# Exponentials of half the heads straight from PSUM, with the negated row maximum as bias, in every attention tile

## The chip, the core and the metric

The kernel runs on one core of a Trainium2 chip. Five engines work side by side, each through its own queue of instructions in order: TensorE (PE in the rows; PEld is its loading of weights), VectorE (DVE), ScalarE (ACT), GpSimd (POOL) and SyncE (SP), which here issues most transfers. They wait for each other by semaphores. The metric is the device time of one execution in microseconds, taken as a median of runs.

## The reference

A recurrent attention layer (gated linear attention, in chunks) is followed by two layers of local attention, each with a feed-forward part. The change touches the softmax of the local attention alone, here cut to what matters (16 windows of 64 rows in each of 2 batches, 8 heads of 64):

```python
q = l2norm(q) * qs; k = l2norm(k) * ksc
q, k = rotary_xpos(q, k)
sim = jnp.einsum('bhwid,bhwjd->bhwij', bq, bk)          # 64 queries against 128 keys
sim = jnp.where(mask, -jnp.finfo(sim.dtype).max, sim)
attn = jax.nn.softmax(sim, axis=-1)
out = jnp.einsum('bhwij,bhwjd->bhwid', attn, bv)
x = x + out_of_all_heads @ wo
```

So for each row of scores the kernel needs the row's maximum, exp(score - maximum), the sum of these, and their product with the values. The row sum comes from a column of ones beside the values, and the division by it stands after the product.

## The kernel before

The 2 x 1024 rows are 16 tiles of 128 rows (`NT` = 16, the batches alternating). A tile `n` has 8 heads of 128 keys, so a row of scores has 1024 numbers: heads of `a = 0` in one bank of PSUM (512 columns, 4 heads), those of `a = 1` in the next; together they are `p_sc`. Weights and activations stay in SBUF throughout. `N = base + n` counts the tiles of both layers (`base` is 0 or 16).

The attention of a layer is a software pipeline written by hand. In step `k` each engine runs its list `attn_step`, and each entry works on a tile with its own lag: `scores` of tile k, the projection of tile k + 2, the transposes of queries and keys of k + 1, the output projection of k - 1, and so on. `staged(fn, k, parity, lag)` drops an entry whose tile doesn't exist. The order in the list is the order in the engine's queue, and nothing reorders it. Layer 0 enters the pipeline with step 3, since its tiles 0 to 2 are interleaved by hand with the end of the recurrent stage (`recurrent_stage_and_first_tiles`). In layer 1, step 0 is written out by hand on ScalarE, interleaved with the end of layer 0's feed-forward part. `drain` ends a layer: it holds tiles 14 and 15 and the first blocks of the feed-forward part.

The way of one tile through the softmax, before:

- TensorE, `scores` (L925): masks and products into `p_sc`.
- VectorE, `row_max` (L2099): two reductions of 128x512, one for each `a`, negated, into `neg_max`.
- VectorE, `subtract_max` (L2106): two additions `probs <- p_sc + neg_max` (PSUM to SBUF, 128x512 each).
- ScalarE, `exponentials` (L1438): two ACTIVATEs of 128x512 in place in `probs`, one for each `a`.
- TensorE, `transpose_probs` (L957): 16 transposes back into `p_sc`, the first 8 for `a = 0` and the last 8 for `a = 1`, each half behind its exponentials (`p_ready`).
- ScalarE, `copy_probs_t` (L1454) to SBUF; TensorE, `weigh_values` (L970); VectorE, `row_reciprocals` and `normalise_o` (`o_n`); TensorE, `transpose_o` (L986); ScalarE, `copy_o_t` (`o_t`).

ScalarE's list for step k, from the place that matters: `copy_o_t` of tile k - 1, `copy_h_t` of k + 3 (two small copies, only while tile k + 3 exists, so up to k = 12), the two exponentials of k, `copy_qk_t` of k + 1 (the transposed queries and keys), `copy_probs_t` of k, `squares` of k + 2 (`sq`), `copy_v_cur`, small work of the normalisation, and in the next step `ln_of_squares` and `inverse_norms`. VectorE's list: `normalise_o` of k - 1, two `row_max`, two `subtract_max`, `rotate` of k + 2 (two products with the tables, which read the projection), `add_attention`, the statistics of z, `sum_squares` of k + 2 (waits for `sq`), `row_reciprocals` of k, `bound_squares`.

There is a second form already. For the last tile of each layer, in `drain`, ScalarE runs `exponentials_of_scores` (L1444), which reads the scores of `a = 0` in PSUM head by head and takes the negated maximum as the instruction's bias; VectorE then subtracts for `a = 1` alone:

```python
for c in range(PAIRS):
    at = (par * AH + c) * P
    ins = act.activation(probs[:, at:at + P], p_sc[:, c * P:(c + 1) * P], ACT.Exp, bias=neg_max[:, c:c + 1])
```

Of the kernel before, what the change touches and what calls it, by code (L numbers as in the profile page):

```python
# [8 lines left out]
ALU = mybir.AluOpType  # L9
# [3 lines left out]
P = 128  # L13
# [4 lines left out]
def wait(engine, semaphore, count):  # L18

    if isinstance(count, int) and count <= 0:  # L20
        return
    engine.wait_ge(semaphore, count)


def build_program(nc, x, Wq, Wk, Wv, Wg, Wgk1, Wgk2, bgk2, Wo, rms_w,
# [26 lines left out]
    with ctx:  # L52
# [604 lines left out]
        def _(pe):  # L657
# [211 lines left out]
            for l in range(DEPTH):  # L869
# [86 lines left out]

                def transpose_probs(n, par):  # L957
                    N = base + n
                    wait(pe, s["sub_ready"], 2 * N + 2)
                    for a in range(2):  # L960
                        wait(pe, s["p_ready"], 2 * N + a + 1)
                        for c in range(PAIRS):
                            i = a * PAIRS + c
                            at = (par * AH + i) * P
                            for w in range(2):
                                r = slice(w * W, (w + 1) * W)
                                ins = pe.transpose(p_sc[:, w * 512 + i * W:w * 512 + (i + 1) * W], probs[r, at:at + P], ident[r, r])  # L967
                    ins.then_inc(s["pt_done"], 1)
# [271 lines left out]
        def _(act):  # L1240
# [157 lines left out]
            for l in range(DEPTH):  # L1398
# [36 lines left out]
                                   p_turn[:, :].rearrange("p (w c k) -> p w c k", w=2, k=W), ACT.Copy  # L1435
                                   ).then_inc(s["qkt_ready"], 1)

                def exponentials(n, par, a):  # L1438
                    N = base + n
                    wait(act, s["sub_ready"], 2 * N + a + 1)  # L1440
                    p = probs[:, par * AH * P + a * 512:par * AH * P + (a + 1) * 512]
                    act.activation(p, p, ACT.Exp).then_inc(s["p_ready"], 1)  # L1442

                def exponentials_of_scores(n, par):  # L1444
# [48 lines left out]
                def attn_step(k, par):  # L1493
                    staged(ln_of_squares, k, par, 1)
                    staged(inverse_norms, k, par, 1)
                    staged(copy_o_t, k, par, -1)
                    if k + 3 > 1:
                        staged(copy_h_t, k, par, 3)
                    staged(exponentials, k, par, 0, 0)
                    staged(exponentials, k, par, 0, 1)  # L1500
                    staged(copy_qk_t, k, par, 1)
                    staged(copy_probs_t, k, par, 0)
                    staged(squares, k, par, 2)
                    staged(copy_v_cur, k, par, 1)
                    staged(ln_of_z, k, par, -2)
                    staged(rstd_of_z, k, par, -2)
                    staged(copy_z_t, k, par, -3)

                def drain():
                    k, last = NT - 2, NT - 1  # L1510
                    ln_of_squares(last, 1)
                    inverse_norms(last, 1)
                    copy_o_t(k - 1, 1)
                    exponentials(k, 0, 0)
                    exponentials(k, 0, 1)
                    copy_qk_t(last, 1)
                    copy_probs_t(k, 0)
                    copy_v_cur(last, 1)
                    ln_of_z(k - 2, 0)
                    rstd_of_z(k - 2, 0)  # L1520
                    copy_z_t(k - 3, 1)
                    exponentials_of_scores(last, 1)
                    exponentials(last, 1, 1)
                    copy_probs_t(last, 1)
                    copy_o_t(k, 0)
                    act.preload_act_table_set("gelu_and_others")
                    gelu_block(l, 0, 0)
                    gelu_block(l, 0, 1)
                    copy_o_t(last, 1)
                    gelu_block(l, 0, 2)  # L1530
                    gelu_block(l, 1, 0)
                    copy_z_t(last - 3, 0)
                    gelu_block(l, 1, 1)
                    copy_z_t(last - 2, 1)
                    gelu_block(l, 1, 2)
                    copy_z_t(last - 1, 0)
                    copy_z_t(last, 1)

                def recurrent_stage_and_first_tiles():
# [184 lines left out]
                    squares(2, 0)  # L1724
                    gla_copy_o_t(7, 1)
                    rstd_of_f(5, 1)
                    exponentials(0, 0, 0)
                    copy_h_t(4, 0)
                    exponentials(0, 0, 1)
                    copy_qk_t(1, 1)  # L1730
                    copy_probs_t(0, 0)
                    ln_of_squares(2, 0)
# [3 lines left out]
                    squares(3, 1)  # L1736
                    ln_of_y(7, 1)
                    rstd_of_y(7, 1)
                    exponentials(1, 1, 0)
                    copy_o_t(0, 0)  # L1740
                    exponentials(1, 1, 1)
                    ln_of_f(7, 1)
                    copy_qk_t(2, 0)
                    copy_probs_t(1, 1)
# [4 lines left out]
                    copy_h_t(5, 1)  # L1749
                    squares(4, 0)  # L1750
                    copy_o_t(1, 1)
                    exponentials(2, 0, 0)
                    exponentials(2, 0, 1)
                    copy_qk_t(3, 1)
                    copy_probs_t(2, 0)
                    ln_of_z(0, 0)
# [3 lines left out]
                if l:  # L1760
                    feed_forward(l - 1, range(2, NG), {(NG - 2, 1): (lambda: copy_h_t(0, 0),), (NG - 1, 0): (lambda: copy_h_t(1, 1),),
                                                       (NG - 1, 2): (lambda: squares(0, 0),)})
                    act.preload_act_table_set("natural_log_exp_and_others")
                    ln_of_squares(0, 0)
                    inverse_norms(0, 0)
                    squares(1, 1)
                    copy_qk_t(0, 0)
                    copy_h_t(2, 0)
                    ln_of_squares(1, 1)
                    inverse_norms(1, 1)  # L1770
                    copy_v_cur(0, 0)
                    copy_h_t(3, 1)
                    exponentials(0, 0, 0)
                    exponentials(0, 0, 1)
                    copy_qk_t(1, 1)
                    copy_probs_t(0, 0)
                    squares(2, 0)
                    copy_v_cur(1, 1)
                else:
                    recurrent_stage_and_first_tiles()  # L1780
# [32 lines left out]
        def _(dve):  # L1813
# [249 lines left out]
            for l in range(DEPTH):  # L2063
# [35 lines left out]
                def row_max(n, par, a):  # L2099
                    N = base + n  # L2100
                    wait(dve, s["sc_done"], N + 1)
                    wait(dve, s["sub_ready"], 2 * (N - 1) + a + 1)
                    dve.tensor_reduce(neg_max[:, a * PAIRS:(a + 1) * PAIRS], heads_of(p_sc, a), AX.X, ALU.max, negate=True  # L2103
                                      ).then_inc(s["max_ready"], 1)

                def subtract_max(n, par, a, halves=1):  # L2106
                    N = base + n
                    wait(dve, s["max_ready"], 2 * N + a + 1)
                    wait(dve, s["pt_done"], N - 1)
                    dve.tensor_tensor(heads_of(probs, a, par * AH * P), heads_of(p_sc, a),  # L2110
                                      neg_max[:, a * PAIRS:(a + 1) * PAIRS].unsqueeze(2).to_broadcast([P, PAIRS, P]), ALU.add
                                      ).then_inc(s["sub_ready"], halves)

                def weighed(at, cols):

# [36 lines left out]
                def attn_step(k, par):  # L2152
                    staged(normalise_o, k, par, -1)
                    staged(row_max, k, par, 0, 0)
                    staged(row_max, k, par, 0, 1)
                    staged(subtract_max, k, par, 0, 0)
                    staged(subtract_max, k, par, 0, 1)
                    staged(rotate, k, par, 2)
                    staged(add_attention, k, par, -1)
                    staged(stats_z, k, par, -2)  # L2160
                    staged(aggregate_z, k, par, -2)
                    staged(sum_squares, k, par, 2)
                    staged(row_reciprocals, k, par, 0)
                    staged(bound_squares, k, par, 2)
# [11 lines left out]
                def drain():  # L2176
# [1 line left out]
                    normalise_o(k - 1, 1)  # L2178
                    row_max(k, 0, 0)
                    row_max(k, 0, 1)  # L2180
                    subtract_max(k, 0, 0)
                    subtract_max(k, 0, 1)
                    stats_z(k - 2, 0)
                    aggregate_z(k - 2, 0)
                    row_max(last, 1, 0)
                    row_max(last, 1, 1)
                    subtract_max(last, 1, 1, 2)
                    row_reciprocals(k, 0)
                    normalise_o(k, 0)
                    add_attention(k - 1, 1)  # L2190
# [16 lines left out]
                def recurrent_stage_and_first_tiles():  # L2207
# [141 lines left out]
                    row_max(0, 0, 0)  # L2349
                    dve.wait_ge(s["gate_ready"], NP)  # L2350
                    dve.wait_ge(s["kv_done"], NP)
                    subtract_max(0, 0, 0)
                    row_max(0, 0, 1)
                    subtract_max(0, 0, 1)
                    stats_f(6, 0)
                    sum_squares(2, 0)
                    aggregate_f(6, 0)
# [5 lines left out]
                    normalise_o(0, 0)  # L2363
                    row_max(1, 1, 0)
                    normalise_y(7, 1)
                    subtract_max(1, 1, 0)
                    row_max(1, 1, 1)
                    subtract_max(1, 1, 1)
                    stats_f(7, 1)
                    aggregate_f(7, 1)  # L2370
                    sum_squares(3, 1)
# [5 lines left out]
                    row_max(2, 0, 0)  # L2377
                    row_reciprocals(1, 1)
                    normalise_o(1, 1)
                    subtract_max(2, 0, 0)  # L2380
                    row_max(2, 0, 1)
                    subtract_max(2, 0, 1)
                    sum_squares(4, 0)
                    stats_z(0, 0)
                    aggregate_z(0, 0)
# [83 lines left out]
```

## Time and profile before

| | |
|---|---|
| median of 3 runs | 425.06 us (424.95 to 425.51) |
| the profiled execution | 425.17 us, its span 423.4 us |
| busy, share of the span | PE 94%, DVE 80%, ACT 72%, POOL 68% |
| granted TensorE clock, mean over the span | 0.999 |
| attention of layer 0 with the recurrent stage | 0 to about 217 us |
| attention of layer 1 | from about 257 to 383 us |

The span runs from the first to the last instruction; the profiled execution's own time has 1.8 us around it. Busy shares are averages over stages with different limits, so the rows below are timelines. A timeline row gives the start, the length of the whole row, the engine, the line, the operation, its output and inputs, and how many instructions it merges; behind it stands the idle time of the engine before it and what ended that. Instructions of one engine overlap a little at their ends, so two merged ones are shorter than the sum of both.

### The profile page before, as it was taken

Reading aid. Unit: us, or ns where it says so; the run is one execution under the profiler, and the core shown is the slowest. Engines: PE = TensorE matmul, PEld = TensorE weight load, DVE = VectorE, ACT = ScalarE, POOL = GpSimd, SP = SyncE. Lnnn points to the kernel's source line nnn. Section 1 sums busy time; section 2 is a strip of 40 time slices with the busy share of each in tenths; the row PEclk is TensorE's granted clock in tenths of the full one; section 3 lists DMA queues with packets and bytes.
Section 4 is the critical chain, followed back from the end, with each engine's and each line's share of the span. In section 5 each row is a group of like instructions: output and inputs, shape, how many; then the busy total and the mean of one; then the engine's idle time right before and its main releaser. Section 6 shows DMA issues by size and latency. Waiting matters only on the chain. (4 is left out here: it accounts for less than half of the span.)

```text
span 423.4 us, 14239 instructions
## 1 busy us (share of the span) xinstructions
PE 398.1 (94%) x5363; PEld 270.5 (64%) x5363; DVE 338.3 (80%) x717; ACT 304.0 (72%) x658; POOL 289.0 (68%) x284
## 2 busy tenths in 40 slices
PE   5989999899899999999989998999999999999994
PEld 2657666456676676776666665667767676666563
DVE  4887777899889999989745377899899899864676
ACT  3868877867868888887874347778878878875424
POOL 2576799899778788777713536677777778761425
PEclk9999999999999999999999999999999999999999
DMA  7840000000000000000000000000000000000012
GB/s 192 310 105 3 4 3 2 2 2 4 8 14 9 11 13 8 10 13 10 8 9 13 0 2 2 8 9 10 12 10 8 13 11 8 11 8 14 6 39 62
DMA packets 21058, 10.44 MB, mean 25 GB/s; under 512 B 13252, under 2 KB 20224, under 8 KB 20992
## 3 DMA queue, kind: packets, MB, share of 16 engines
q1 hardware_dynamic: 20384, 9.32, 8.1%
q8 instruction: 44, 0.72, 0.7%
q10 hardware_dynamic: 608, 0.21, 0.2%
q14 instruction: 22, 0.18, 0.1%
HBM read 6.38 MB, written 1.05 MB: 18 GB/s over the span
## 5 line engine op out<-in xcount | busy, mean ns | idle before, releaser
L461 POOL TENSOR_TENSOR qr<-rot 128x1024 f32<-128x1024 f32 x32 | 75.8, 2370 | 28.3 <-DVE rot L2075 23.7
L659 PE MATMUL psum<-wqkv_sb,h_t 128*128 128x512 f32 x192 | 93.8, 598 | 0.7 <-issue 0.4
L469 POOL TENSOR_TENSOR qr<-qr,inv 128x1024 f32<-128x1024 f32 x32 | 60.8, 1901 | 27.7 <-ACT inv L1426 27.7
L2083 DVE TENSOR_REDUCE ss<-sq 128x16 f32<-128x1024 f32 x32 | 38.9, 1217 | 15.1 <-ACT sq L1415 15.1
L2103 DVE TENSOR_REDUCE neg_max<-psum 128x4 f32<-128x512 f32 x64 | 41.4, 685 | 4.4 <-PE psum L659 4.2
L659 PE MATMUL psum<-z_t,w_sb 128*128 128x512 f32 (+1 forms) x96 | 44.8, 595 | 0.0
L1442 ACT ACTIVATE probs<-probs 128x512 f32<-128x512 f32 x62 | 38.2, 631 | 7.7 <-DVE probs L2110 5.6
L659 PEld LDWEIGHTS psum<-wqkv_sb,h_t 128*128 128x128 f32 x192 | 31.6, 191 | 18.2 <-issue 17.8
L2075 DVE TENSOR_TENSOR rot<-psum,cos_t 128x1024 f32<-128x1024 f32 x32 | 39.1, 1223 | 3.0 <-PE psum L659 2.1
L659 PEld LDWEIGHTS psum<-v_mix,probs_t 128*64 128x64 f32 x512 | 32.2, 138 | 14.0 <-issue 14.0
L1386 ACT ACTIVATE gelu<-psum,columns 128x512 f32<-128x512 f32 (+1 forms) x24 | 16.4, 685 | 34.4 <-PE psum L659 34.4
L2110 DVE TENSOR_TENSOR probs<-psum,neg_max 128x512 f32<-128x512 f32 x62 | 40.0, 682 | 0.4
L659 PE MATMUL psum<-v_mix,probs_t 128*64 128x65 f32 x512 | 36.5, 224 | 2.6 <-ACT probs_t L1458 2.6
L2075 DVE TENSOR_TENSOR rot<-psum,sin_t 128x1024 f32<-128x1024 f32 x32 | 38.8, 1214 | 0.0
L2048 DVE SCALAR_TENSOR_TENSOR hid<-psum,columns,gelu 128x512 f32<-128x512 f32 (+1 forms) x24 | 18.0, 749 | 24.1 <-ACT gelu L1386 24.1
L659 PE MATMUL psum<-v_cur,probs_t 128*64 128x65 f32 x512 | 36.7, 225 | 0.0
L1415 ACT ACTIVATE sq<-psum 128x1024 f32<-128x1024 f32 x32 | 33.0, 1031 | 5.1 <-DVE rot L2075 5.1
L659 PE MATMUL psum<-wo_sb,o_t 128*128 128x128 f32 x256 | 36.7, 286 | 0.0
L1464 ACT ACTIVATE o_t<-psum 128x512 f32<-128x512 f32 x32 | 19.1, 596 | 22.7 <-PE psum L992 21.3
L659 PE MATMUL psum<-qk_t 64*64 64x128 f32 x1024 | 33.5, 269 | 0.0
L1458 ACT ACTIVATE probs_t<-psum 128x1024 f32<-128x1024 f32 x32 | 32.6, 1018 | 1.2 <-PE psum L967 1.2
L922 PEld LDWEIGHTS psum<-consts,qr 64*128 64x128 f32 x512 | 18.5, 139 | 23.3 <-POOL qr L469 20.3
(157 smaller groups left out, 934.0 us busy)
## 6 DMA issues: line engine op xcount, KB each, us to landing
wqkv_sb<-in_L_ffn_wqkv SPq DMA_DIRECT2D x1, 1536.0 KB, 9.8
hcat<-middle SPq DMA_DIRECT2D x32, 32.0 KB
hcat<-middle SPq DMA_DIRECT2D x32, 31.8 KB
out_x<-pong SPq DMA_DIRECT2D x7, 128.0 KB, 1.8
x_in<-in_L_attn_x SPq DMA_DIRECT2D x2, 384.0 KB, 4.8
w_sb<-in_L_ffn_w SPq DMA_DIRECT2D x1, 682.0 KB
cos_base<-rotary_cos SPq DMA_DIRECT2D x1, 512.0 KB, 5.1
sin_base<-rotary_sin SPq DMA_DIRECT2D x1, 512.0 KB, 6.2
```

Source lines behind the costliest of these rows:

```text
L461: pool.tensor_tensor(o, a, b[:, :, ::-1, :], ALU.add).then_inc(s["add_ready"], 1)
L469: pool.tensor_tensor(a, a, inv[:, :].unsqueeze(2).to_broadcast([P, 2 * AH, DH]), ALU.mult).then_inc(s["qr_ready"], 1)
L659: return pe.matmul(o, w, m, start=start, stop=stop, skip_group_check=skip)
L922: ins = pe.transpose(p_turn[:, w * 512 + c * W:w * 512 + (c + 1) * W], qr[r, at:at + P], ident[r, r])
L1415: act.activation(sq[:, :], p_qk[:, :], ACT.Square).then_inc(s["sq_ready"], 1)
L1442: act.activation(p, p, ACT.Exp).then_inc(s["p_ready"], 1)
L1458: act.activation(probs_t[:, :], p_sc[:, :], ACT.Copy).then_inc(s["pt_ready"], 1)
L1464: act.activation(o_t[:, :], p_vo[:, :], ACT.Copy).then_inc(s["ot_ready"], 1)
L2075: ins = dve.tensor_tensor(o[:, :].rearrange("p (i h e) -> p i h e", i=2, e=DH), x, tab.unsqueeze(2).to_broadcast([P, 2, AH, DH]), ALU.mult)
L2083: dve.tensor_reduce(ss[:, 0:4 * AH:2], sq[:, :].rearrange("p (h e) -> p h e", e=DH), AX.X, ALU.add).then_inc(s["ss_ready"], 1)
L2103: dve.tensor_reduce(neg_max[:, a * PAIRS:(a + 1) * PAIRS], heads_of(p_sc, a), AX.X, ALU.max, negate=True).then_inc(s["max_ready"], 1)
L2110: dve.tensor_tensor(heads_of(probs, a, par * AH * P), heads_of(p_sc, a), neg_max[:, a * PAIRS:(a + 1) * PAIRS].unsqueeze(2).to_broadcast([ ...
```

## The change

In 30 of the 32 tiles (all but the last of each layer, which had it) the first half of the heads takes the second form. ScalarE's `exponentials` for `a = 0` gives way to `exponentials_of_scores`: four ACTIVATEs of 128x128 from PSUM, which wait for the first maximum (`max_ready` >= 2N + 1) and no subtraction. VectorE's `subtract_max` for `a = 0` is gone; the one that is left waits for the second maximum, which stands right ahead of it. `sub_ready` now counts once a tile, and the first `row_max` of a tile waits for the previous tile's first half of exponentials, which read `neg_max`.

```diff
                 def transpose_probs(n, par):
                     N = base + n
-                    wait(pe, s["sub_ready"], 2 * N + 2)
+                    wait(pe, s["sub_ready"], N + 1)
...
-                def exponentials(n, par, a):
-                    N = base + n
-                    wait(act, s["sub_ready"], 2 * N + a + 1)
-                    p = probs[:, par * AH * P + a * 512:par * AH * P + (a + 1) * 512]
+                def exponentials(n, par):
+                    N = base + n
+                    wait(act, s["sub_ready"], N + 1)
+                    p = probs[:, par * AH * P + 512:(par + 1) * AH * P]
                     act.activation(p, p, ACT.Exp).then_inc(s["p_ready"], 1)
...
-                    staged(exponentials, k, par, 0, 0)
-                    staged(exponentials, k, par, 0, 1)
+                    staged(exponentials_of_scores, k, par, 0)
+                    staged(exponentials, k, par, 0)
...
                 def row_max(n, par, a):
                     N = base + n
                     wait(dve, s["sc_done"], N + 1)
-                    wait(dve, s["sub_ready"], 2 * (N - 1) + a + 1)
+                    if a == 0:
+                        wait(dve, s["p_ready"], 2 * (N - 1) + 1)
+                    else:
+                        wait(dve, s["sub_ready"], N)
...
-                def subtract_max(n, par, a, halves=1):
-                    N = base + n
-                    wait(dve, s["max_ready"], 2 * N + a + 1)
+                def subtract_max(n, par):
+                    N = base + n
+                    wait(dve, s["max_ready"], 2 * N + 2)
                     wait(dve, s["pt_done"], N - 1)
-                    dve.tensor_tensor(heads_of(probs, a, par * AH * P), heads_of(p_sc, a),
-                                      neg_max[:, a * PAIRS:(a + 1) * PAIRS].unsqueeze(2).to_broadcast([P, PAIRS, P]), ALU.add
-                                      ).then_inc(s["sub_ready"], halves)
+                    dve.tensor_tensor(heads_of(probs, 1, par * AH * P), heads_of(p_sc, 1),
+                                      neg_max[:, PAIRS:2 * PAIRS].unsqueeze(2).to_broadcast([P, PAIRS, P]), ALU.add
+                                      ).then_inc(s["sub_ready"], 1)
...
-                    staged(subtract_max, k, par, 0, 0)
-                    staged(subtract_max, k, par, 0, 1)
+                    staged(subtract_max, k, par, 0)
```

The hand-written places change in the same way. In tiles 0 to 2 of layer 0 VectorE had run maximum, subtraction, maximum, subtraction, with other work between; now both maxima come first.

ScalarE in a step of layer 0, around the exponentials; `h_t` is the transposed input of tile k + 3. Before:

```order
L1464 ACTIVATE o_t<-psum 128x512
L1407 ACTIVATE h_t<-psum 64x128
L1408 ACTIVATE h_t<-psum 64x128
L1442 ACTIVATE probs<-probs 128x512 x2
L1434 ACTIVATE qk_t<-psum 128x2x8x64
```

After:

```order
L1464 ACTIVATE o_t<-psum 128x512
L1407 ACTIVATE h_t<-psum 64x128
L1408 ACTIVATE h_t<-psum 64x128
L1451 ACTIVATE probs<-psum,neg_max 128x128 x4
L1442 ACTIVATE probs<-probs 128x512
L1434 ACTIVATE qk_t<-psum 128x2x8x64
```

One instruction of 512 columns has become four of 128, at the same place, between the `h_t` copies and `qk_t`.

VectorE in a step of layer 0, from `o_n` of the tile before to the rotation. Before:

```order
L2130 TENSOR_TENSOR o_n<-psum,row_rec 128x2x4x64
L2103 TENSOR_REDUCE neg_max<-psum 128x4 x2
L2110 TENSOR_TENSOR probs<-psum,neg_max 128x512 x2
L2075 TENSOR_TENSOR rot<-psum,cos_t 128x1024
L2075 TENSOR_TENSOR rot<-psum,sin_t 128x1024
```

After:

```order
L2133 TENSOR_TENSOR o_n<-psum,row_rec 128x2x4x64
L2106 TENSOR_REDUCE neg_max<-psum 128x4 x2
L2113 TENSOR_TENSOR probs<-psum,neg_max 128x512
L2075 TENSOR_TENSOR rot<-psum,cos_t 128x1024
L2075 TENSOR_TENSOR rot<-psum,sin_t 128x1024
```

The rotation stands one subtraction nearer to the maxima. TensorE's and POOL's orders are the same as before.

## Rows read from the trace of the kernel before

**Rows 1.** busy time by stretch: start:end, length, PE, PEld, DVE, ACT, POOL, PEclk, DMA

```profile
80.00:100.00 20.00, 17.57 (x237) 10.66 (x236) 19.00 (x37) 15.19 (x36) 19.25 (x17) 1.00 0.01 2
300.00:320.00 20.00, 20.00 (x284) 13.84 (x283) 18.74 (x32) 17.27 (x35) 15.92 (x14) 1.00 0.04 9
```

**Rows 2.** timeline of ScalarE, one step of layer 1: start us, length us, engine, line

```profile
316.29 0.60 ACT L1464 ACTIVATE o_t<-psum 128x512 f32<-128x512 f32 x1 [0.78 <-PE psum L992]
...
317.06 0.27 ACT L1408 ACTIVATE h_t<-psum 64x128 f32<-64x128 f32 x1
317.44 1.23 ACT L1442 ACTIVATE probs<-probs 128x512 f32<-128x512 f32 x2
318.69 1.02 ACT L1434 ACTIVATE qk_t<-psum 128x1024 f32<-128x1024 f32 x1
...
320.52 1.03 ACT L1415 ACTIVATE sq<-psum 128x1024 f32<-128x1024 f32 x1
...
324.39 0.60 ACT L1464 ACTIVATE o_t<-psum 128x512 f32<-128x512 f32 x1 [0.78 <-PE psum L992]
```

**Rows 3.** timeline of TensorE, the same step

```profile
315.60 0.66 PE L992 MATMUL psum<-consts,o_n 128*128 128x128 f32 x4
316.09 1.88 PE L659 MATMUL psum<-wqkv_sb,h_t 128*128 128x512 f32 x4
317.90 0.72 PE L922 MATMUL psum<-consts,qr 64*128 64x64 f32 x16
318.45 0.73 PE L967 MATMUL psum<-consts,probs 64*128 64x64 f32 x16
...
323.70 0.66 PE L992 MATMUL psum<-consts,o_n 128*128 128x128 f32 x4
```

**Rows 4.** timeline of VectorE, the same step

```profile
315.52 1.29 DVE L2103 TENSOR_REDUCE neg_max<-psum 128x4 f32<-128x512 f32 x2
316.73 1.28 DVE L2110 TENSOR_TENSOR probs<-psum,neg_max 128x512 f32<-128x512 f32 x2
318.01 1.23 DVE L2075 TENSOR_TENSOR rot<-psum,cos_t 128x1024 f32<-128x1024 f32 x1
...
321.58 1.22 DVE L2083 TENSOR_REDUCE ss<-sq 128x16 f32<-128x1024 f32 x1 [0.56 <-ACT sq L1415]
...
322.95 0.69 DVE L2130 TENSOR_TENSOR o_n<-psum,row_rec 128x512 f32<-128x512 f32 x1
```

**Rows 5.** timeline of VectorE, last tile of layer 0

```profile
213.67 1.29 DVE L2103 TENSOR_REDUCE neg_max<-psum 128x4 f32<-128x512 f32 x2 [1.97 <-PE psum L659]
215.05 0.69 DVE L2110 TENSOR_TENSOR probs<-psum,neg_max 128x512 f32<-128x512 f32 x1
```

**Rows 6.** groups by line and shape, ScalarE: count, busy us, mean ns, idle before

```profile
L1442 ACT ACTIVATE probs<-probs 128x512 f32<-128x512 f32 x62 | 38.2, 631 | 7.7 <-DVE probs L2110 5.6
...
L1451 ACT ACTIVATE probs<-psum,neg_max 128x128 f32<-128x128 f32 x8 | 2.3, 368 | 1.9 <-DVE neg_max L2103 1.9
```

**Rows 7.** timeline of ScalarE, last tile of layer 0

```profile
214.40 1.14 ACT L1451 ACTIVATE probs<-psum,neg_max 128x128 f32<-128x128 f32 x4 [0.97 <-DVE neg_max L2103]
```

**Rows 8.** timeline of ScalarE, tile 0 of layer 1

```profile
260.43 0.27 ACT L1408 ACTIVATE h_t<-psum 64x128 f32<-64x128 f32 x1
260.73 1.15 ACT L1442 ACTIVATE probs<-probs 128x512 f32<-128x512 f32 x2
262.14 1.02 ACT L1434 ACTIVATE qk_t<-psum 128x1024 f32<-128x1024 f32 x1 [0.27 <-PE psum L922]
```

**Rows 9.** timeline of ScalarE, k = 14 of layer 1, without `h_t` copies

```profile
372.96 0.60 ACT L1464 ACTIVATE o_t<-psum 128x512 f32<-128x512 f32 x1 [0.78 <-PE psum L992]
...
375.32 1.03 ACT L1434 ACTIVATE qk_t<-psum 128x1024 f32<-128x1024 f32 x1
```

**Rows 10.** timeline of ScalarE, tile 2 of layer 0

```profile
112.32 1.29 ACT L1442 ACTIVATE probs<-probs 128x512 f32<-128x512 f32 x2
113.52 1.01 ACT L1434 ACTIVATE qk_t<-psum 128x1024 f32<-128x1024 f32 x1
```

More of the change, by code:

```diff
@@ L1513, in drain @@
                     copy_o_t(k - 1, 1)
-                    exponentials(k, 0, 0)
-                    exponentials(k, 0, 1)
+                    exponentials_of_scores(k, 0)
+                    exponentials(k, 0)
                     copy_qk_t(last, 1)
@@ L1522, in drain @@
                     exponentials_of_scores(last, 1)
-                    exponentials(last, 1, 1)
+                    exponentials(last, 1)
                     copy_probs_t(last, 1)
@@ L1726, in recurrent_stage_and_first_tiles @@
                     rstd_of_f(5, 1)
-                    exponentials(0, 0, 0)
+                    exponentials_of_scores(0, 0)
                     copy_h_t(4, 0)
-                    exponentials(0, 0, 1)
+                    exponentials(0, 0)
                     copy_qk_t(1, 1)
@@ L1738, in recurrent_stage_and_first_tiles @@
                     rstd_of_y(7, 1)
-                    exponentials(1, 1, 0)
+                    exponentials_of_scores(1, 1)
                     copy_o_t(0, 0)
-                    exponentials(1, 1, 1)
+                    exponentials(1, 1)
                     ln_of_f(7, 1)
@@ L1751, in recurrent_stage_and_first_tiles @@
                     copy_o_t(1, 1)
-                    exponentials(2, 0, 0)
-                    exponentials(2, 0, 1)
+                    exponentials_of_scores(2, 0)
+                    exponentials(2, 0)
                     copy_qk_t(3, 1)
@@ L1772, in _ @@
                     copy_h_t(3, 1)
-                    exponentials(0, 0, 0)
-                    exponentials(0, 0, 1)
+                    exponentials_of_scores(0, 0)
+                    exponentials(0, 0)
                     copy_qk_t(1, 1)
@@ L2180, in drain @@
                     row_max(k, 0, 1)
-                    subtract_max(k, 0, 0)
-                    subtract_max(k, 0, 1)
+                    subtract_max(k, 0)
                     stats_z(k - 2, 0)
@@ L2186, in drain @@
                     row_max(last, 1, 1)
-                    subtract_max(last, 1, 1, 2)
+                    subtract_max(last, 1)
                     row_reciprocals(k, 0)
@@ L2351, in recurrent_stage_and_first_tiles @@
                     dve.wait_ge(s["kv_done"], NP)
-                    subtract_max(0, 0, 0)
                     row_max(0, 0, 1)
-                    subtract_max(0, 0, 1)
+                    subtract_max(0, 0)
                     stats_f(6, 0)
@@ L2365, in recurrent_stage_and_first_tiles @@
                     normalise_y(7, 1)
-                    subtract_max(1, 1, 0)
                     row_max(1, 1, 1)
-                    subtract_max(1, 1, 1)
+                    subtract_max(1, 1)
                     stats_f(7, 1)
@@ L2379, in recurrent_stage_and_first_tiles @@
                     normalise_o(1, 1)
-                    subtract_max(2, 0, 0)
                     row_max(2, 0, 1)
-                    subtract_max(2, 0, 1)
+                    subtract_max(2, 0)
                     sum_squares(4, 0)
```

## The prediction

> **What bounds the kernel now.** The view of busy time by stretches comes first. In the steady attention stretch TensorE is busy for all of 20 us and VectorE and ScalarE for 18.74 and 17.27 [rows 1], so shares alone don't say which one sets the pace. The timelines of one step (step k = 7 of layer 1) do. I call the first `o_t` copy of a step time 0; it starts at 316.29 and the next at 324.39, so a step takes 8.10 us [rows 2].
>
> Follow it round. ScalarE starts `o_t` 0.03 after TensorE ends the four transposes of `o_n` (315.60 + 0.66) [rows 3]. ScalarE then copies `h_t` twice, takes both halves' exponentials from 317.44, and copies `qk_t` at 318.69, which is time 2.40. `probs_t` follows, then `sq` at 320.52 [rows 2]. VectorE's sum of squares has idled 0.56 for that `sq` and starts 0.03 after its end; `o_n` follows, and ends at 323.64 [rows 4]. TensorE transposes it 0.06 later, at 323.70 [rows 3]. Every link of this ring is tight, and it crosses three engines. That TensorE is nearly full at the same time is the balance of a tuned kernel, not slack elsewhere.
>
> What holds the exponentials inside the ring? The first subtraction ends at 316.73 + 0.69 = 317.42 (a single one takes 0.69) [rows 4, 5]; the exponential starts 0.02 later, 0.11 after the second `h_t` copy ends (317.06 + 0.27) [rows 2]. So VectorE holds it, but ScalarE's own queue stands only 0.1 us behind. `qk_t` has a second floor: TensorE's transposes of queries and keys end at 317.90 + 0.72 = 318.62 [rows 3], so `qk_t` could start no earlier than about 2.37.
>
> **What goes away.** In 30 of the 32 tiles VectorE loses one subtraction. Two take 1.28, so one is worth some 0.64 [rows 4]. In the steady step this is worth nothing: the next VectorE instruction is the rotation, which starts at 318.01, just after TensorE's projection of queries and keys (316.09 + 1.88 = 317.97) [rows 3, 4], so the freed time turns into a wait for TensorE. The subtraction that stays must now wait for the maximum right ahead of it. At the end of a layer this form exists already: the pair of maxima starts at 213.67, the one subtraction at 215.05, and it takes 0.69 [rows 5], which is 2.07 from the pair's start. In the steady step that is 315.52 + 2.07 = 317.59, time 1.30. It is needed at 2.10 (below), so this wait has 0.8 us of cover.
>
> **What is added.** ScalarE's first half (mean 631 ns) becomes four instructions of mean 368 ns [rows 6]. The last tile of a layer runs exactly these: four in 1.14 us [rows 7], so they start (1.14 - 0.368) / 3 = 0.257 apart. Four hold ScalarE's queue for 4 x 0.257 = 1.03 us; the half that they replace held it for 1.23 - 0.63 = 0.60 [rows 2, 6]. That is +0.43 us of queue a tile.
>
> In the Trainium skill, the page "ScalarE: Activation LUTs", section "What ACT_TABLE_LOAD costs", says that a bias read through a pointer costs about 93 ns more in each instruction, and that neighbours overlap by about 93 ns. By its figures four of 128 columns would take, as an estimate, 0.29 us each from start to start, 1.18 us in all: 0.15 more a step than the trace's 0.257 apart, and some 435.5 us as the end of the sum below. The trace's four are cheaper, and the sum goes by them.
>
> **How early can the four start?** They no longer wait for a subtraction, only for the first maximum, which ends near 315.52 + 0.64 = 316.2 [rows 4], before `o_t` even starts. So ScalarE's queue decides, behind the second `h_t` copy. The step of tile 0 in layer 1 shows that succession with nothing else to wait for: the copy starts at 260.43, the exponential at 260.73, which is 0.30 later [rows 8]. In the steady step the copy starts at 0.77, so the four start at 1.07 (now 1.15). This gives back 0.08. The bounds: 0.17 behind the copy if these copies overlapped as `sq` and its neighbour could (not seen behind an `h_t` copy), 0.30 as seen. I take 0.30.
>
> **The steady step, summed.** Four exponentials from 1.07, the second half from 1.07 + 1.03 = 2.10, `qk_t` 0.60 later at 2.70 instead of 2.40: **+0.30 us**. The rest of the ring, `qk_t` to the next `o_t`, keeps its length. The other way round, through TensorE, agrees: the second half of the exponentials ends at 2.10 + 0.63 = 2.73, and TensorE would reach the transposes of that half (the last 8 of 16) at 318.45 + 0.33 = 318.78, time 2.49 [rows 3]; it waits some 0.29 with the usual 0.05 for the signal. So both ways lengthen by the same 0.3, and the step goes from 8.10 to 8.40. Behind it everything shifts together: POOL's scaling and rotation hang on the same `sq` and on the projection, and keep their places.
>
> **Which steps pay.** Those that copy an `h_t` ahead of the exponentials: k = 3 to 12 of layer 0 and k = 1 to 12 of layer 1, **22 x 0.30 = 6.6 us**.
> - Tile 0 of layer 1: the four from 260.73, the half from 261.76, `qk_t` at 262.36 instead of 262.14 [rows 8]: +0.2.
> - k = 13 and 14 of both layers have no `h_t` copy. `o_t` starts at 372.96 and `qk_t` at 375.32, time 2.36 [rows 9]. The four could start 0.49 behind `o_t`, `qk_t` at 0.49 + 1.03 + 0.60 = 2.12; TensorE's floor of 2.37 stays. **0** for these four steps.
> - The last tile of a layer already has this form: 0.
> - Tiles 0 to 2 of layer 0 run beside the recurrent stage, where VectorE is busy for 19.00 of 20 us and POOL for 19.25 [rows 1]. Freeing 3 x 0.64 = 1.9 us of VectorE could gain as much, or nothing while POOL is as full. I take 0 for tiles 0 and 1, as POOL is the fuller. At tile 2 both exponentials start at 112.32 and `qk_t` at 113.52 [rows 10]; the four cost 0.43 there, of which I give back 0.13 for the relieved VectorE: +0.3, with bounds from -1.9 to +0.4 for the three tiles.
>
> Sum: 6.6 + 0.2 + 0.3 = **+7.1 us**. The profiled execution took 425.17 (its span 423.4 and 1.8 around it), so 432.3; it stood 0.11 above the median of the runs, which makes **432.2 us**, 1.7% slower. TensorE will idle about 0.3 us in 8.4. Its clock should not suffer: with 17.57 of 20 us busy the granted clock was 1.00, the 2.4 GHz level [rows 1].
>
> **Bounds.** Low: the four start 0.13 earlier in the 22 steps, -2.9, and the first tiles gain 0.7 more than taken: 428.6. High: nothing overlaps at the two seams (the four hold the queue for their whole 1.14, the half for its whole 0.63), +0.14 in 22 steps, 3.1 more: 435.3.
>
> **Rivals.**
> - *Dearer exponentials.* In the steady step, beside a full VectorE, the four could overlap less than at a layer's end. Without overlap at the two seams it is the high bound, 435.3; without any, 4 x 0.368 = 1.47, 0.44 more a step, 22 x 0.74 + 0.5 = 16.8, 442.0. Against it: the four of the last tile ran while VectorE worked on maximum and subtraction (213.67 to 215.74) [rows 5, 7]. 0.12 for the first, 0.04 for the second. The Trainium skill's price of the bias pointer, above, points to the first.
> - *Hidden after all, no change.* ScalarE is idle for 2.73 of 20 us [rows 1], 1.1 a step, more than the 0.43 added. If the added time fell into that idleness, the result would be 425. Against it: that idleness comes after `sq`, in waits for VectorE and for the transposes (0.78 at 324.39) [rows 2], which themselves wait for `sq`. They move; they don't shrink. It would take an `o_n` that waits for something else. 0.06.
> - *Faster.* VectorE is the real bound: the subtraction holds the exponentials by 0.1 now, and in the first tiles it is nearly full. This decides if the four and the half reach `qk_t` by 2.37, so if they hold the queue for 1.30 instead of 1.63 us: then each of 22 steps gains 0.03 and the first tiles up to 1.9, giving 422.6 to 424.2. For it: VectorE has the heavier load, 18.74 against 17.27. Against it: the four would have to start 0.18 apart, against 0.257 seen [rows 6, 7]. 0.05.
> - That the change doesn't do what it says is excluded by the order of ScalarE's instructions, which has the four in each of these tiles.
>
> **How the numbers follow.** My forecast has 0.73, dearer exponentials 0.12 and 0.04, no change 0.06, faster 0.05. The range 428.5 to 435.5 takes in both bounds, so the forecast and about half of the 0.12: 0.8. A measurement of this kernel tells about 0.2%, 0.9 us, from no change, so: faster 0.05, same 0.06, slower 0.89.
>
> **What would show it.** Right: steps 8.4 us apart by the `o_t` copies for k = 3 to 12 and 1 to 12, but 8.1 behind k = 13; the first of four exponentials 0.30 behind the second `h_t` copy; four in 1.14; `qk_t` at 2.70; VectorE's rotation waiting some 0.6 us for TensorE; TensorE waiting about 0.3 us for the exponentials in each step. Wrong: `sq` no longer what the sum of squares waits for; steps of 8.06 to 8.10; four exponentials in 1.4 us; or a first stretch to tile 3 of layer 0 that is shorter by a us or more.

## The result: 431.7 us, 1.5% slower

The changed kernel takes 431.69 us (median of 4 runs, 430.47 to 433.1) against 425.28 us for the kernel before beside it. The ratio is 1.0154, with a 95% interval of 1.0129 to 1.0179. The forecast was 432.2 with a range of 428.5 to 435.5. The profiled execution took 431.64 us, its span 429.8.

**The profile after.** One steady step on ScalarE in the changed kernel (step k = 7 of layer 1, the one that [rows 2] show of before; start us, length us, engine, line, operation):

```profile
321.44 0.60 ACT L1464 ACTIVATE o_t<-psum 128x512 f32<-128x512 f32 x1 [0.80 <-PE psum L992]
...
322.20 0.27 ACT L1408 ACTIVATE h_t<-psum 64x128 f32<-64x128 f32 x1
322.50 1.14 ACT L1451 ACTIVATE probs<-psum,neg_max 128x128 f32<-128x128 f32 x4
323.52 0.65 ACT L1442 ACTIVATE probs<-probs 128x512 f32<-128x512 f32 x1
324.04 1.04 ACT L1434 ACTIVATE qk_t<-psum 128x1024 f32<-128x1024 f32 x1
...
325.85 1.06 ACT L1415 ACTIVATE sq<-psum 128x1024 f32<-128x1024 f32 x1
...
329.77 0.60 ACT L1464 ACTIVATE o_t<-psum 128x512 f32<-128x512 f32 x1 [0.80 <-PE psum L992]
```

From `o_t` to `o_t` it is 8.33 us where it was 8.10. The first of the four exponentials starts 0.30 behind the second `h_t` copy, at time 1.06. The second half starts at 2.08, and `qk_t` at 2.60 where it was 2.40. That is the loss, in one place: +0.20 up to `qk_t`, and +0.03 in the rest of the ring.

VectorE in the same step, which answers to [rows 4]:

```profile
322.10 0.69 DVE L2113 TENSOR_TENSOR probs<-psum,neg_max 128x512 f32<-128x512 f32 x1
323.16 1.22 DVE L2075 TENSOR_TENSOR rot<-psum,cos_t 128x1024 f32<-128x1024 f32 x1 [0.36 <-PE psum L659]
...
326.94 1.22 DVE L2083 TENSOR_REDUCE ss<-sq 128x16 f32<-128x1024 f32 x1 [0.42 <-ACT sq L1415]
...
328.31 0.69 DVE L2133 TENSOR_TENSOR o_n<-psum,row_rec 128x512 f32<-128x512 f32 x1
```

One subtraction is left, and the rotation now waits 0.36 us for TensorE: the saved time became a wait. The sum of squares still waits for `sq`, for 0.42 us.

TensorE in the same step, which answers to [rows 3]:

```profile
320.80 0.60 PE L992 MATMUL psum<-consts,o_n 128*128 128x128 f32 x4
...
323.05 0.71 PE L922 MATMUL psum<-consts,qr 64*128 64x64 f32 x16
323.79 0.89 PE L967 MATMUL psum<-consts,probs 64*128 64x64 f32 x16
...
329.13 0.60 PE L992 MATMUL psum<-consts,o_n 128*128 128x128 f32 x4
```

The 16 transposes of probabilities (L967) took 0.73 and now take 0.89, and they begin at 323.79, 0.03 after the transposes ahead of them end; before, they overlapped them by 0.17. Both fit a wait for exponentials that come later: the first half of them ends at 323.64 and the second at 324.17. The work behind these transposes starts at time 3.17 (324.61), where it started at 2.83 (319.12), 0.34 later.

The last steps of a layer, without an `h_t` copy, answer to [rows 9]:

```profile
371.41 0.60 ACT L1464 ACTIVATE o_t<-psum 128x512 f32<-128x512 f32 x1 [0.77 <-PE psum L992]
...
379.47 0.60 ACT L1464 ACTIVATE o_t<-psum 128x512 f32<-128x512 f32 x1 [0.78 <-PE psum L992]
379.97 1.14 ACT L1451 ACTIVATE probs<-psum,neg_max 128x128 f32<-128x128 f32 x4
380.97 0.66 ACT L1442 ACTIVATE probs<-probs 128x512 f32<-128x512 f32 x1
381.84 1.03 ACT L1434 ACTIVATE qk_t<-psum 128x1024 f32<-128x1024 f32 x1 [0.22 <-PE psum L922]
```

There `o_t` to `o_t` is 8.06, as before. The four start 0.50 behind `o_t`, the half is done early, and `qk_t` waits 0.22 for TensorE, to stand at time 2.37.

The view of busy time for 20 us of the steady stretch, which answers to [rows 1], with the same columns, shows VectorE down from 18.74 to 16.71. TensorE is at 19.95 where it was at 20.00, so its wait of 0.34 us a step hardly shows in the busy time:

```profile
300.00:320.00 20.00, 19.95 (x302) 13.96 (x305) 16.71 (x32) 17.48 (x41) 14.93 (x11) 1.00 0.05 11
```

### The profile page after: what moved, and what is told of

It is laid out like the page before. It is cut to its first block, busy times and chain, and to the rows that moved or that the text cites. A ratio compares the mean times of both kernels' runs of the same rounds, so it can differ in the third digit from the quotient of the medians.

```text
span 429.8 us, 14299 instructions
## 1 busy us (share of the span) xinstructions
PE 403.9 (94%) x5363; PEld 273.1 (64%) x5363; DVE 324.7 (76%) x687; ACT 314.5 (73%) x748; POOL 289.4 (67%) x284
## 4 chain that ended last, share of the span: by engine, by line
PE 59%; ACT 6%; POOL 6%; issue 6%; DVE 2%; POOLq 0%; ACTq 0%; DVEq 0%
PE psum L659 46%; PE psum L967 5%; PE psum L922 4%; PE psum L992 3%; ACT probs_t L1458 2%; PE psum L893 1%; POOL qr L461 1%; ACT sq L1415 1%; ACT qk_t L1434 1%; POOL ping L443 1%; POOL qr L469 1%; PE psum L1012 1%; ACT probs L1442 1%; DVE o_n L2133 1%; ACT probs L1451 1%
## 5 line engine op out<-in xcount | busy, mean ns | idle before, releaser
L1451 ACT ACTIVATE probs<-psum,neg_max 128x128 f32<-128x128 f32 x128 | 36.6, 370 | 2.9 <-DVE neg_max L2106 2.4
L1434 ACT ACTIVATE qk_t<-psum 128x1024 f32<-128x1024 f32 x32 | 33.2, 1036 | 0.9 <-PE psum L922 0.9
```

Of the source, the lines that this page charges most:

```text
L1434: act.activation(qk_t[:, at:at + 2 * INNER].rearrange("p (c w k) -> p w c k", w=2, k=W), p_turn[:, :].rearrange("p (w c k) -> p w c k", w= ...
```

## Experiments

Theory Q is the prediction's: the loss is the time for which four small instructions hold ScalarE's queue between the `h_t` copies and `qk_t`. It says where the loss should vanish (fewer instructions, or other work moved out of that place), where it should grow, and that VectorE's part is worth nothing. Each rival is named in the expectation that it belongs to.

### One exponential of 512 columns in place of four

The maxima of heads 1 to 3 are left out here: head 0's serves all four. PSUM as the source and the pointer as the bias stay.

```diff
-                    for c in range(PAIRS):
-                        at = (par * AH + c) * P
-                        ins = act.activation(probs[:, at:at + P], p_sc[:, c * P:(c + 1) * P], ACT.Exp, bias=neg_max[:, c:c + 1])
-                    ins.then_inc(s["p_ready"], 1)
+                    at = par * AH * P
+                    act.activation(probs[:, at:at + 512], p_sc[:, 0:512], ACT.Exp, bias=neg_max[:, 0:1]
+                                   ).then_inc(s["p_ready"], 1)
```

> The changed kernel with the four exponentials of 128 columns replaced by one of 512 columns, which still reads PSUM and still takes a pointer as its bias (it leaves out the maxima of heads 1 to 3: head 0's serves all four). Theory Q (the loss is the time that four instructions hold ScalarE's queue between the h_t copies and qk_t, 0.255 us each): one instruction holds it for about 0.58 instead of 1.02, qk_t falls back on TensorE's floor (2.37 behind o_t instead of 2.60), steps of 8.06 instead of 8.33: 22 x 0.27 + 0.4 = 6.3 us less than the changed kernel, about 425.4. Rival P (the loss comes from reading PSUM on ScalarE, or from the VectorE side, not from the count of instructions): no change, 431.7.

Measured: 425.05 us, ratio to the kernel before 0.9985 (0.9946 to 1.0023). One step on ScalarE in this kernel:

```profile
308.33 0.60 ACT L1463 ACTIVATE o_t<-psum 128x512 f32<-128x512 f32 x1 [0.77 <-PE psum L992]
...
309.09 0.27 ACT L1408 ACTIVATE h_t<-psum 64x128 f32<-64x128 f32 x1
309.39 0.69 ACT L1450 ACTIVATE probs<-psum,neg_max 128x512 f32<-128x512 f32 x1
309.98 0.62 ACT L1442 ACTIVATE probs<-probs 128x512 f32<-128x512 f32 x1
310.69 1.02 ACT L1434 ACTIVATE qk_t<-psum 128x1024 f32<-128x1024 f32 x1
...
316.39 0.60 ACT L1463 ACTIVATE o_t<-psum 128x512 f32<-128x512 f32 x1 [0.78 <-PE psum L992]
```

The one instruction holds the queue for 0.59 us (309.39 to 309.98). `qk_t` starts at time 2.36, 0.09 after the half ends: ScalarE is free by then, and the time is that of TensorE's floor. Steps are 8.06 us. The loss is gone with PSUM, the pointer and VectorE's side unchanged, so rival P is out. For the same 512 columns, what costs is the count of instructions.

### Two more exponentials of 128 columns

```diff
+                    for c in range(2):
+                        at = (par * 2 + c) * P
+                        act.activation(spare[:, at:at + P], p_sc[:, c * P:(c + 1) * P], ACT.Exp, bias=neg_max[:, c:c + 1])
                     for c in range(PAIRS):
```

> The changed kernel with two further exponentials of 128 columns ahead of the four in every tile, written to a spare buffer that nobody reads. Theory Q: 2 x 0.255 = 0.51 more on the ring in each of 22 steps, 11.2; in k = 13 and 14 qk_t goes from 2.37 to 2.54, 4 x 0.17 = 0.7; tile 0 of layer 1, tiles 0 to 2 of layer 0 and the last tiles some 2 together: 14 us more than the changed kernel, 445.6, steps of 8.84. Rival S (the steps are paced by something that only happens to be near, and ScalarE has idle time to spend): at most 5 us more, 436.7.

Measured: 444.87 us, ratio 1.0442 (1.0385 to 1.0498). One step on ScalarE:

```profile
307.82 0.60 ACT L1468 ACTIVATE o_t<-psum 128x512 f32<-128x512 f32 x1 [0.80 <-PE psum L993]
...
308.89 0.63 ACT L1452 ACTIVATE spare<-psum,neg_max 128x128 f32<-128x128 f32 x2
309.40 1.14 ACT L1455 ACTIVATE probs<-psum,neg_max 128x128 f32<-128x128 f32 x4
310.40 0.66 ACT L1443 ACTIVATE probs<-probs 128x512 f32<-128x512 f32 x1
310.92 1.06 ACT L1435 ACTIVATE qk_t<-psum 128x1024 f32<-128x1024 f32 x1
...
316.67 0.60 ACT L1468 ACTIVATE o_t<-psum 128x512 f32<-128x512 f32 x1 [0.80 <-PE psum L993]
```

Two more take 0.51 (308.89 to 309.40) and the step is 8.85, against 8.84 expected. With one, four and six instructions the steps are 8.06, 8.33 and 8.85. Above TensorE's floor every 0.255 us on ScalarE's queue is paid in full, so rival S is out: ScalarE's idle time doesn't take any of it.

### VectorE's subtraction put back

A subtraction of the same size, ahead of the one that is left, writes to a spare buffer. It reads the scores of `a = 1`, since the bank of `a = 0` is being read by ScalarE.

```diff
                     wait(dve, s["pt_done"], N - 1)
+                    if n < LAST:
+                        dve.tensor_tensor(heads_of(spare, par), heads_of(p_sc, 1),
+                                          neg_max[:, PAIRS:2 * PAIRS].unsqueeze(2).to_broadcast([P, PAIRS, P]), ALU.add)
```

> The changed kernel with one more subtraction of 128x512 on VectorE in each of the 30 tiles, ahead of the one that is left, written to a spare buffer: VectorE's saved work is put back while ScalarE's stays as changed. Theory Q says that the saved 0.6 us of VectorE is worth nothing in the steady steps (it became a wait of 0.36 us for TensorE, and the rotation's end has 0.3 us of cover): 431.7 to 432.2. Rival V (the relief of VectorE pays back part of ScalarE's cost in each step): 22 x 0.2 to 0.6, 436 to 445.

Measured: 431.87 us, ratio 1.015 (1.0084 to 1.0216), which can't be told from the changed kernel's 431.69. VectorE in one step:

```profile
304.84 0.69 DVE L2115 TENSOR_TENSOR spare<-psum,neg_max 128x512 f32<-128x512 f32 x1
305.45 0.68 DVE L2117 TENSOR_TENSOR probs<-psum,neg_max 128x512 f32<-128x512 f32 x1
306.05 1.21 DVE L2076 TENSOR_TENSOR rot<-psum,cos_t 128x1024 f32<-128x1024 f32 x1
...
309.68 1.22 DVE L2084 TENSOR_REDUCE ss<-sq 128x16 f32<-128x1024 f32 x1 [0.42 <-ACT sq L1416]
```

The extra subtraction fills what was a wait for TensorE, and the rotation follows it directly. The sum of squares starts 0.42 after VectorE's last work, waiting for `sq` as before, and the step stays at 8.33 (`o_t` at 304.18 and 312.51). Rival V is out for the steady steps. In k = 13 and 14, where ScalarE is early, the extra subtraction does show: 8.23 instead of 8.06, so there VectorE's relief is cover that is needed, though no gain over the kernel before.

### Tiles 0 to 2 of layer 0 in the old form

```diff
+                    subtract_first(0, 0)
                     row_max(0, 0, 1)
...
-                    exponentials_of_scores(0, 0)
+                    exponentials_first(0, 0)
```

The same was done for tiles 1 and 2. The two new functions are the subtraction and the exponential for `a = 0` as they stood before.

> The changed kernel with the old form (two subtractions, two exponentials of 512 columns) in tiles 0 to 2 of layer 0 alone, beside the recurrent stage. Theory Q: tile 2's lengthened queue is gone, 0.3 to 0.4 less, 431.3. Rival V (the relief of VectorE was worth up to 1.9 us there): up to 1.9 more, 433.6.

Measured: 431.47 us, ratio 1.0119 (1.0074 to 1.0164): the medians can't tell it from the changed kernel. The timelines can. `qk_t` of tile 0 and `o_t` of step 3, in the kernel before, in the changed kernel and in this one:

```profile
89.17 1.00 ACT L1434 ACTIVATE qk_t<-psum 128x1024 f32<-128x1024 f32 x1
...
118.70 0.60 ACT L1464 ACTIVATE o_t<-psum 128x512 f32<-128x512 f32 x1 [1.84 <-PE psum L992]
```

```profile
89.78 1.01 ACT L1434 ACTIVATE qk_t<-psum 128x1024 f32<-128x1024 f32 x1
...
119.70 0.60 ACT L1464 ACTIVATE o_t<-psum 128x512 f32<-128x512 f32 x1 [1.84 <-PE psum L992]
```

```profile
89.90 1.00 ACT L1434 ACTIVATE qk_t<-psum 128x1024 f32<-128x1024 f32 x1
...
119.44 0.60 ACT L1469 ACTIVATE o_t<-psum 128x512 f32<-128x512 f32 x1 [1.84 <-PE psum L992]
```

Between them lie 29.53, 29.92 and 29.54 us. So these three tiles cost 0.39 us in the changed kernel, and VectorE's relief beside the recurrent stage, where it had been busy for 19.00 of 20 us [rows 1], brought no net gain. The kernel with the subtraction put back says the same: there it is 29.90 us (89.12 to 119.02), so the relief alone is worth 0.02.

### The `h_t` copies moved to the end of the step

If the four instructions only cost because of their place, the place can be emptied. The copies of `h_t` move behind `z_t`, where ScalarE waits anyway. Two waits of TensorE for `h_t` are set one tile earlier, and a wait for `add_attention` keeps the two readers of that PSUM bank apart.

```diff
-                    if k + 3 > 1:
-                        staged(copy_h_t, k, par, 3)
                     staged(exponentials_of_scores, k, par, 0)
...
                     staged(copy_z_t, k, par, -3)
+                    staged(copy_h_t_late, k, par, 3)
```

> The changed kernel, four exponentials kept, with the two h_t copies moved on ScalarE from between o_t and the exponentials to the end of the step (behind z_t, where ScalarE waits for VectorE and TensorE anyway). Theory Q: the four start 0.49 behind o_t instead of 1.06, qk_t could start at 2.03 and so falls back on TensorE's floor of 2.37; steps of 8.06 to 8.10 instead of 8.33, 22 x 0.25 = 5.5 us less, 426.0, which is the kernel before within 0.2%. Rival W (ScalarE is simply too full: what is added must be paid somewhere in the step): steps stay at 8.3, 431.7.

Measured: 425.27 us, ratio to the kernel before 0.9992 (0.9959 to 1.0026). One step on ScalarE:

```profile
308.92 0.60 ACT L1468 ACTIVATE o_t<-psum 128x512 f32<-128x512 f32 x1 [0.57 <-PE psum L992]
309.41 1.14 ACT L1455 ACTIVATE probs<-psum,neg_max 128x128 f32<-128x128 f32 x4
...
311.28 1.03 ACT L1438 ACTIVATE qk_t<-psum 128x1024 f32<-128x1024 f32 x1 [0.21 <-PE psum L922]
...
316.98 0.60 ACT L1468 ACTIVATE o_t<-psum 128x512 f32<-128x512 f32 x1 [0.56 <-PE psum L992]
```

The four run 0.57 us earlier, `qk_t` waits 0.21 for TensorE and stands at time 2.36, and steps are 8.06. All four exponentials are still there and the loss of the steady steps is gone, so rival W is out: ScalarE had the time, but in another place.

### The same move in the kernel before

> The kernel before with the same move of the h_t copies, as the control. Theory Q: there VectorE's two subtractions held the exponentials, not ScalarE's queue, and TensorE's floor stands 0.03 below: at most 22 x 0.03 = 0.7 us less, 424.6 to 425.3. Rival C (the h_t copies cost ring time in any form, so the move is worth the same in both kernels): 5 us less, 420.

The diff is the one above, on the old lists. Measured: 425.41 us, ratio 0.9981 (0.995 to 1.0013). One step on ScalarE:

```profile
308.49 0.60 ACT L1468 ACTIVATE o_t<-psum 128x512 f32<-128x512 f32 x1 [0.57 <-PE psum L992]
309.68 1.23 ACT L1446 ACTIVATE probs<-probs 128x512 f32<-128x512 f32 x2 [0.59 <-DVE probs L2113]
310.86 1.02 ACT L1438 ACTIVATE qk_t<-psum 128x1024 f32<-128x1024 f32 x1
...
316.55 0.60 ACT L1468 ACTIVATE o_t<-psum 128x512 f32<-128x512 f32 x1 [0.57 <-PE psum L992]
```

The exponentials start at time 1.19, no earlier than the 1.15 of [rows 2], although nothing of ScalarE's own is in their way: they idle 0.59 for VectorE's subtraction. Steps are 8.06 to 8.10. The move is worth nothing here, and rival C is out. In the kernel before ScalarE's queue was covered by VectorE; the change took that cover away and lengthened the queue.

### Both reliefs at once

Late `h_t` copies and the one exponential of 512 columns (again head 0's maximum for four heads).

> Both reliefs at once: h_t copies late and one exponential of 512 columns in place of the four (head 0's maximum for four heads, the other three left out). Theory Q with a floor at 2.37: ScalarE reaches qk_t at 1.6, but must wait for TensorE; the same as with the late copies alone within 0.3%, 425 to 426, steps of 8.06. Rival N (no floor: every 0.1 us off ScalarE's queue pays): 22 x 0.43 = 9 us less than with the late copies alone, 417.

Measured: 424.73 us, ratio 0.9967 (0.9936 to 0.9997). One step on ScalarE:

```profile
308.58 0.60 ACT L1467 ACTIVATE o_t<-psum 128x512 f32<-128x512 f32 x1 [0.57 <-PE psum L992]
309.07 0.68 ACT L1454 ACTIVATE probs<-psum,neg_max 128x512 f32<-128x512 f32 x1
...
310.95 1.02 ACT L1438 ACTIVATE qk_t<-psum 128x1024 f32<-128x1024 f32 x1 [0.49 <-PE psum L922]
...
316.64 0.60 ACT L1467 ACTIVATE o_t<-psum 128x512 f32<-128x512 f32 x1 [0.57 <-PE psum L992]
```

ScalarE now waits 0.49 for TensorE before `qk_t`, which stands at 2.37 all the same, and steps are 8.06. Rival N is out: the floor is real. The 0.5 us below the kernel with late copies alone is about what the first tiles give back (from `qk_t` of tile 0 to `o_t` of step 3 it is 29.53 here and 29.95 there). No version in this study that keeps each head's own maximum beats the kernel before by more than can be measured.

## Why the prediction was right, and where it was off

- **The ring and the engine that ends last: right.** The prediction had the ring run through ScalarE, VectorE and TensorE, and ScalarE's own queue 0.1 us behind VectorE. The control with the late copies shows that VectorE held it before, and the runs with one, four and six instructions show that ScalarE holds it after.
- **The step: +0.23, not +0.30.** The term that was mis-sized is the second half of the exponentials. The prediction took 0.60 us for the time from it to `qk_t`, from the pair in [rows 2]. In the pair the second half had started 0.60 behind the first because it waited for the second subtraction (316.73 + 1.28 = 318.01, and 317.44 + 0.60 = 318.04). Freed of that, it holds the queue for 0.52 (323.52 to 324.04). The pair of [rows 8], which takes 1.15 instead of 1.23 with nothing to wait for, had shown it. The other terms held: 0.30 behind the `h_t` copy, 1.02 for the four against 1.03, the half's end at time 2.73.
- **TensorE's way round: right in kind.** The prediction let TensorE wait some 0.29 us for the exponentials and gave both ways the same length. The work behind the transposes comes 0.34 later. In the step after, `o_n` ends at 328.31 + 0.69 = 329.00 and its transposes start at 329.13, 0.13 behind it instead of 0.06, so the way through TensorE is now the longer by some 0.07. At `o_t` 0.02 of that is left (0.77 behind `o_n` instead of 0.75), since the four transposes take 0.60 instead of 0.66.
- **VectorE's wait: 0.36, not 0.6.** The sign that the prediction named doesn't follow from its own rows, in which the one subtraction ends at 317.59 and the rotation starts at 318.01, 0.42 later. The saved time did become a wait, and the run with the subtraction put back shows that it is worth nothing in the steady steps.
- **Which steps pay: right.** k = 13 and 14 pay nothing, on TensorE's floor of 2.37. From `o_t` of step 3 to that of step 13 layer 0 took 81.11 us before and 83.70 after, and layer 1 from step 1 to 13 97.05 and 99.93, so 5.5 us in 22 steps instead of 6.6. One of them (8.72 us, with 0.17 of TensorE's wait for `o_n`) is an isolated step; without its 0.39 it is 5.1, or 0.23 a step. Every kernel here that reads the scores from PSUM in the first half shows one or two such steps, at other sizes, and the two kernels in the old form show none behind the first step (8.21 in the kernel before). What causes it stays open.
- **Tiles 0 to 2: +0.39 against +0.3, in part by luck.** Tile 2 cost what the prediction gave it: from one `qk_t` to the next 7.90 us before (105.62 to 113.52) and 8.23 after (106.26 to 114.49). Tiles 0 and 1 were taken as 0 each. Tile 0 gained 0.29 (7.56 to 7.27) and tile 1 lost 0.32 (8.89 to 9.21). In tile 1 VectorE waits for POOL twice, 0.57 us at 98.13 and 0.95 at 105.25, where it had not waited before. This fits the prediction's argument that POOL is the fuller; that it took the gain back is not shown.
- **Tile 0 of layer 1: +0.12 against +0.2.** `qk_t` starts 1.83 us behind the second `h_t` copy (263.94 to 265.77), before 1.71. It is the same mis-sized term, the 0.60 of the second half.
- **The total is closer than its terms.** The steps account for 5.5, the first tiles for 0.4, tile 0 of layer 1 for 0.1, and 0.6 was already there at `qk_t` of tile 0 (89.78 against 89.17), before any instruction that the change touches. Together that is 6.6 of the 6.4 us by which the span grew; the stretches between them are 0.2 shorter. The profiles of the other kernels with the changed form stand between 89.12 and 89.90 at that point, the one with subtractions put back below the kernel before. So the 0.6 is put down to the execution and not to the change, though no kernel has two traces to show it; the interval of the result, 5.5 to 7.6 us, holds 5.8 as well as 6.4. With six exponentials, whose profiled execution took 448.24 us, it is 92.92: there the granted clock was 0.50, the 1.2 GHz level, from 26 to 32 us, and 1.00 in the changed kernel's first 100 us. The shorter steps (1.1 less than forecast) and the later start (0.6 more) partly cancelled, so that the total came within 0.5 of the forecast is in part luck.
- **The rivals.** "Hidden after all" is out by the result and by the run with six exponentials, "faster" by the result and by the run with the subtraction put back. Dearer exponentials did not occur: the four took 1.14 in the steady step as at a layer's end. The Trainium skill's price for the bias pointer ("ScalarE: Activation LUTs", section "What ACT_TABLE_LOAD costs", some 0.093 us an instruction) gives more than the rows show. By its figures four of 128 columns would start some 0.29 apart, as an estimate; their mean length is 370 ns and they start 0.255 apart:

```profile
L1451 ACT ACTIVATE probs<-psum,neg_max 128x128 f32<-128x128 f32 x128 | 36.6, 370 | 2.9 <-DVE neg_max L2106 2.4
```

  With 512 columns the pointer's instruction holds the queue for 0.59 against 0.52 for the plain one, 0.07 more. The plain one reads SBUF and the other PSUM, so no run here shows the pointer's price by itself.
- **The clock.** TensorE's granted clock stayed at 1.00, the 2.4 GHz level, in the steady stretch, as the prediction said.

## What to carry to other kernels

In this kernel moving work from one busy engine to another was worth what the ring of waits got back, not what the busy shares suggest: VectorE had the larger load, but its saved time turned into a wait, while ScalarE's added time stood where each microsecond counted. Before splitting one instruction into several, look at what stands ahead of them in their queue. In this kernel the same four instructions cost 5 us behind two copies and nothing in the steady steps once the copies had moved into ScalarE's idle time. When a duration is read from a row that merges two instructions, ask first whether the second one waited.

## What the runs showed of the hardware

On ScalarE the time for which an instruction held the queue was not its length in these traces. A plain exponential of 512 columns from SBUF is 0.65 us long and holds it for 0.52; one from PSUM with a pointer as bias 0.69 and 0.59; one of 128 columns 0.37 and 0.255. The second `h_t` copy (64x128) is 0.27 long and is followed by the next instruction 0.30 after its start, so behind it no overlap was seen. Four instructions of 128 columns hold the queue for 1.02 us and one of 512 for 0.59.
